# Layer 1 of a two-layer attention and mixture-of-experts kernel: where the shared expert's units stand, and when the experts' weights are sent

## The reference

```python
logits = x @ router_w; scores = sigmoid(logits)
# 4 of 8 groups, then 8 of their experts; weights normed, times 2.5
gate = ragged_dot(xs, w_gate, group_sizes)      # tokens sorted by expert
up   = ragged_dot(xs, w_up, group_sizes)
down = ragged_dot(silu(gate) * up, w_down, group_sizes)
routed = (down[unsort].reshape(T, K, H) * tkw[..., None]).sum(axis=1)
shared = silu(x @ sw_gate) * (x @ sw_up) @ sw_down     # width 256 inside
return routed + shared
```

## Time and profile before

| | us |
|---|---|
| three runs | 1168.87, 1170.13, 1175.76 |
| median | 1170.13 |
| the profiled execution, as timed | 1172.08 |
| its span in the profile | 1169.5 |

### The profile page before, as it was taken

The page is one execution under the profiler, slowest core; times in us unless marked ns, Lnnn a source line. Parts: engine busy times, 40 slices in busy tenths (PEclk is TensorE's granted clock), DMA queues, the critical chain, the costliest instruction groups (busy, mean ns, idle before and its releaser), DMA issues.

```text
span 1169.5 us, 22075 instructions
## 1 busy us (share of the span) xinstructions
PE 899.2 (77%) x5927; PEld 691.8 (59%) x5927; DVE 685.6 (59%) x2692; ACT 467.1 (40%) x1176; POOL 621.2 (53%) x870
## 2 busy tenths in 40 slices
PE   1687989878597992379987888856899999989900
PEld 1465667657355881256665565533688887778700
DVE  4678888865532554467687674352455544444568
ACT  2346666743112441257655443311344444444400
POOL 3646666523163652336558888755356655545500
PEclk9859999988798996559989576787999999999955
DMA  8500000000624543400002222566455655545287
GB/s 231 192 2 1 2 2 1 1 2 1 263 106 127 152 130 120 144 1 2 2 29 86 85 97 101 210 222 221 147 163 174 182 157 161 153 141 156 70 327 319
DMA packets 73093, 136.97 MB, mean 117 GB/s; under 512 B 13406, under 2 KB 51725, under 8 KB 70928
## 3 DMA queue, kind: packets, MB, share of 16 engines
q1 hardware_dynamic: 52144, 85.15, 22.8%
q0 software_dynamic: 17632, 46.73, 11.2%
q10 hardware_dynamic: 3200, 3.70, 0.9%
HBM read 79.15 MB, written 62.39 MB: 121 GB/s over the span
## 4 chain that ended last, share of the span: by engine, by line
PE 36%; DVE 9%; POOL 6%; issue 5%; ACT 2%; another core or an unknown queue 1%; DMA 1%; DVEq 0%; POOLq 0%; ACTq 0%; SPq 0%
PE s_psum L1996 12%; PE s_psum L2009 6%; PE s_psum L1988 3%; POOL rows L1553 3%; PE s_psum L1477 3%; PE s_psum L2004 2%; DVE a_masked L1074 2%; DVE f_rows L2096 2%; DVE f_xT L2096 2%; PE s_psum L549 1%; POOL a_probs L1414 1%; PE s_psum L1496 1%; PE s_psum L646 1%; PE s_psum L602 1%
## 5 line engine op out<-in xcount | busy, mean ns | idle before, releaser
L2106 POOL DMA_INDIRECT parts<-e_y,e_dest x206 | 202.7, 984 | 180.7 <-DVE e_y L2079 96.9
L1996 PE MATMUL s_psum<-wres,e_xT 128*128 x824 | 213.9, 382 | 1.8 <-ACT e_xT L2036 1.0
L1996 PEld LDWEIGHTS s_psum<-wres,e_xT 128*128 128x128 f32 x824 | 156.1, 191 | 26.1 <-issue 5.4
L1414 POOL TENSOR_SCALAR_AFFINE_SELECT a_probs<-a_probs 128x256 f32<-128x256 f32 x256 | 107.5, 444 | 117.6 <-ACT a_probs L870 116.8
L1553 POOL DMA_INDIRECT rows<-f_rows,f_place_at x128 | 125.2, 978 | 40.3 <-issue 31.7
L2009 PE MATMUL s_psum<-wres,e_hT 128*128 x412 | 125.3, 386 | 12.2 <-ACT e_hT L2046 11.6
L870 ACT ACTIVATE a_probs<-s_psum 128x768 f32<-128x768 f32 x128 | 104.6, 817 | 72.8 <-PE s_psum L629 68.2
L2041 ACT ACTIVATE e_act_out<-s_psum 128x128 f32<-128x128 f32 x206 | 57.1, 277 | 180.8 <-PE s_psum L1996 101.6
L2070 DVE TENSOR_TENSOR e_hid<-e_act_out,s_psum 128x128 f32<-128x128 f32 x206 | 59.0, 286 | 91.8 <-issue 42.6
L1074 DVE CUSTOM_DVE_ANT_0 a_masked<-s_psum,a_ahead 128x128 f32<-128x128 f32 (+1 forms) x256 | 76.1, 353 | 42.0 <-PE s_psum L605 39.1
L2079 DVE TENSOR_SCALAR e_y<-s_psum,e_xg 128x256 f32<-128x256 f32 x206 | 99.6, 484 | 0.7 <-issue 0.7
(11 more groups left out here) (297 smaller groups left out, 1993.4 us busy)
## 6 DMA issues: line engine op xcount, KB each, us to landing
e_xg<-rows SPq DMA_DIRECT2D x159, 160.0 KB
f_rows<-parts SPq DMA_DIRECT2D x8, 1024.0 KB, 7.2
f_xT<-parts SPq DMA_DIRECT2D x8, 1024.0 KB, 7.4
wres<-in_experts SPq DMA_DIRECT2D x21, 384.0 KB
e_xg<-rows SPq DMA_DIRECT2D x47, 144.0 KB
wres<-in_experts SPq DMA_DIRECT2D x4, 1536.0 KB
rows<-empty SPq DMA_DIRECT2D x1, 5120.0 KB, 24.1
e_yk<-parts SPq DMA_DIRECT2D x16, 256.0 KB, 2.9
```

The lines of the kernel that those rows point to most:

```text
L1414: last = nc.gpsimd.affine_select(out=diagonal[:, :, a], in_=diagonal[:, :, a], compare_op=ALU.is_ge, fill=0.0, base=0, pattern=[[0, 2], [1 ...
L1996: last = nc.tensor.matmul(ps_u[b % 2][:, 0:2 * P], xT[b % 2][:, c * P:(c + 1) * P], wres[:, ds(e, 1), 2 * c * P:2 * (c + 1) * P].rearrange ...
L2106: nc.gpsimd.indirect_dma_start(out=parts[:, :], out_offset=bass.IndirectOffsetOnAxis(ap=dest[b % NY][:], axis=0), in_=y[b % NY][:], in_off ...
```

## The change

- The tables that placed units 0 to 3 in rounds 9 and 10 are gone. `finish` runs units 0 to 3 in place of 4 to 7. `up(0)` and `up(1)` stand ahead of `count`, so ahead of the wait for the last places.
- Units 4 to 7 (`TAIL_UNITS`) run behind the expert loop: PE behind the last block, ACT ahead of the stores, DVE between the sums of the first eight tiles. Tile 8 waits for all units.
- Attention's buffers are ordered anew, so that parts of `wres` come free earlier. SP sends experts 25 to 13 on one count per slot from (7, 0) to (8, 4), and 12 to 0 on one count per four scatters from round 9 on; the last five also wait for all places. The transfer of five at once is gone.
- In rounds 10 and 11 POOL sends one scatter per slot instead of two, so `finish` has 22 scatters left instead of 6.
- `xg` and `y` of the loop now lie in `rows`, and the four `yk` buffers in `wres`, so that `xT` and the shared weights stay for the last units.

```diff
-PACED = 78
+STACK_EXPERTS, FIRST_QUERY_EXPERTS, SECOND_QUERY_EXPERTS = 19, 16, 13
+ROUND_STEPS = 13
+PACE = 4
+TAIL_UNITS = 4
@@ attention
-        unit_pe = {(B + 1, 0): [("up", 0)], (B + 1, 2): [("up", 1)], (B + 1, 3): [("down", 0)], (B + 1, 5): [("down", 1)],
-                   (B + 1, 7): [("up", 2)], (B + 2, 1): [("up", 3)], (B + 2, 2): [("down", 2)], (B + 2, 6): [("down", 3)]}
@@ sync
-                sp.wait_ge(st_ps, PAIRS * B)
-                sp.wait_ge(max_done, PAIRS * B)
-                for n, e in enumerate(range(FREE_EXPERTS - 1, LAST_EXPERTS - 1, -1)):
+                sp.wait_ge(group_ps, NF * B)
+                for n, e in enumerate(range(FREE_EXPERTS - 1, -1, -1)):
+                    if e == STACK_EXPERTS - 1:
+                        sp.wait_ge(st_ps, PAIRS * (B - 2))
+                    if e == FIRST_QUERY_EXPERTS - 1:
+                        sp.wait_ge(st_ps, PAIRS * (B - 1))
+                    if e == SECOND_QUERY_EXPERTS - 1:
+                        sp.wait_ge(st_ps, PAIRS * B)
+                        sp.wait_ge(max_done, PAIRS * B)
+                    if e == LAST_EXPERTS - 1:
+                        sp.wait_ge(f_placed, B)
                     sp.wait_ge(front["paced"], n + 1)
@@ gpsimd
-                        for _ in range(2):
+                        for _ in range(2 if i <= B + 1 else 1):
...
-                            if scattered >= PACED and scattered % 2:
+                            scattered += 1
+                            if i > B and scattered % PACE == 0:
                                 passed(pool, front["paced"])
-                            scattered += 1
+                        if (B - 1, 0) <= (i, j) < (B - 1 + ROUND_STEPS // PAIRS, ROUND_STEPS % PAIRS):
+                            passed(pool, front["paced"])
@@ finish, tensor
+            units["up"](pe, 0)
+            units["up"](pe, 1)
             count()
-            units["up"](pe, begun)
-            first()
-            units["up"](pe, begun + 1)
-            for u in range(begun, NU):
+            for u in range(end):
                 units["down"](pe, u)
-                if u == begun:
+                if u + 2 < end:
+                    units["up"](pe, u + 2)
+                if u == 0:
+                    first()
+                if u == 1:
                     table()
@@ expert_blocks, tensor, behind the loop
+                units["up"](pe, NU - TAIL_UNITS)
+                units["up"](pe, NU - TAIL_UNITS + 1)
+                for u in range(NU - TAIL_UNITS, NU):
+                    units["down"](pe, u)
+                    if u + 2 < NU:
+                        units["up"](pe, u + 2)
@@ expert_blocks, vector, in the loop over tiles t
+                tail = {0: [("keep", u)], 1: [("keep", u + 1)], 2: [("add", u)], 3: [("keep", u + 2)], 4: [("add", u + 1)],
+                        5: [("keep", u + 3)], 6: [("add", u + 2)], 7: [("add", u + 3)]}
             for t in range(NT):
+                for name, u in tail.get(t, []):
+                    units[name](dve, u)
```

More of the change, by code:

```diff
@@ L391, in attention, with query_homes @@
             place_top = sb("place_top", [P, TB, 8])
+        pieces = NH // 2 + (NK // 2 if multi else 1)
+        def query_homes(i):
+            return (sb(f"qT{i}", [P, PAIRS, N], F32R), sb(f"kT{i}", [P, PAIRS if multi else 1, N], F32R))
+        ahead = sb("ahead", [P, TRI])
+        masked = wide("masked", [P, 2, 2, TRI])
+        max_stack = sb("max_stack", [P, TB, 2, 2 * NH, 2], F32R)
+        maxT = sb("maxT", [P, TRI], F32R)
+        pairs_by_age = {i: query_homes(i) for i in (1, 0, 2)}
+        qT, kT = ([pairs_by_age[i][n] for i in range(NQ)] for n in range(2))
         yT_hi = sb("yT_hi", [P, FC, N], F32R)
@@ L1798, in finish @@
     make_sem, psum, block = shared_stage
-    placed, wres_loaded, units, begun = front["placed"], front["wres_loaded"], front["units"], front["units_begun"]
+    placed, units, end = front["placed"], front["units"], NU - TAIL_UNITS
     with ExitStack() as ctx:
@@ L1887, in _ @@
             dve.wait_ge(ones_made, 1)
+            units["keep"](dve, 0)
             dve.wait_ge(count_ps, 1)
@@ L1892, in _ @@
             nc.vector.tensor_copy(blocks[:], blocks_i[:]).then_inc(blocks_done, 1)
-            units["keep"](dve, begun)
+            units["add"](dve, 0)
+            units["keep"](dve, 1)
             dve.wait_ge(blocks_done, 1)
@@ L1903, in _ @@
             nc.vector.tensor_tensor(lists[:, NB:2 * NB], owned[:], start[:], ALU.mult).then_inc(lists_done, 1)
-            units["add"](dve, begun)
+            units["add"](dve, 1)
+            units["keep"](dve, 2)
             dve.wait_ge(tab_ps, 1)
             nc.vector.tensor_copy(tab[0:1, 0:2 * NB], ps_r[0:1, 0:2 * NB]).then_inc(tab_done, 1)
-            for u in range(begun + 1, NU):
+            units["add"](dve, 2)
+            for u in range(3, end):
                 units["keep"](dve, u)
@@ L2018, in _ @@
             if front is not None:
[L2019 removed]
+                pe.wait_ge(front["units"]["added"], NU - TAIL_UNITS)
             for i in range(NB + 2):
@@ L2029, in _ @@
                     down(i - 2, owner.pop(0))
+            if front is not None:
+                units = front["units"]
+                units["up"](pe, NU - TAIL_UNITS)
[4 more added lines that the diff above has]
+                        units["up"](pe, u + 2)
         @block.scalar
@@ L2056, in _ @@
                     keep_hidden(i - 1)
+            if front is not None:
+                for u in range(NU - TAIL_UNITS, NU):
+                    front["units"]["silu"](act, u)
             if out is not None:
@@ L2090, in _ @@
             sums.start(0)
+            tail = {}
+            if front is not None:
+                units, u = front["units"], NU - TAIL_UNITS
+                tail = {0: [("keep", u)], 1: [("keep", u + 1)], 2: [("add", u)], 3: [("keep", u + 2)], 4: [("add", u + 1)],
+                        5: [("keep", u + 3)], 6: [("add", u + 2)], 7: [("add", u + 3)]}
             for t in range(NT):
+                for name, u in tail.get(t, []):
+                    units[name](dve, u)
+                if front is not None and t == NT // 2:
+                    dve.wait_ge(units["added"], NU)
                 part = yk[t % NC]
```

58 lines of the change are left out of this document (18 added, 40 removed).

## The result

The changed kernel takes 1176.49 us (median of 11 runs, 1169.58 to 1187.07), the kernel before 1166.88 (11 runs, 1159.41 to 1175.76). The ratio is 1.0083, with a 95% interval of 1.0044 to 1.0123: slower by 0.8%. A ratio rests only on executions within 1.5% of the fastest of their kernel, so it can differ a little from the quotient of two medians. Forecast were 1168 us and a gain of 2.2 us. The profiled execution of the changed kernel (1169.95 us, span 1167.9) is one of its fastest, that of before (1172.08, span 1169.5) one of the slower. So the two spans, laid side by side, mislead by about 11 us. Stages have to be compared, and several traces of each kernel.

A forecast was written before the change was run, and what follows sets the result against it. Bounds: POOL in rounds 5 to 8, POOL's scatters beside the routing chain in the drain, PE in the expert loop, DVE in the tail. -14.1 + 11.9 = -2.2 us from 1170.13 gave 1168 us, own range 1162 to 1175.

The forecast's parts named there:

- Part 1, the drain: Rounds 9 and 10 without units: last scatter at 808.4 us, not 822.75, 14.4 us earlier, less 1 us of idle.
- POOL never waits: In the drain, POOL issues its 52 remaining scatters without idling, 1.27 us each, 66.2 us in all.
- perhaps two late starts of about 6 us each: On the path to the places of m=7, late ACT and DVE starts that may disappear, 12 us together.
- the places would stand at about 774 us: The places of m=7 come 12 us sooner on a path of 29.7 us, early enough for POOL.
- 786 with the late starts kept: Time in us of the places of m=7 if ACT and DVE still start late; claimed to fit too.
- Part 2, the loads: Weight loads paced one per slot in rounds 7 and 8, then one per four scatters: DMA share about 0.6, cost 0.
- second rival: Rounds 7 and 8 pay for the loads through late PE or ACT starts: 1180 us, or 1186 with three; chance 0.14.
- No stretch of DMA share above 0.9: Sign expected between rounds 9 and 11, where the near-full DMA stretches should go.
- Part 3, the start: Expert loop's first block near 816 us, effectively 817.3 with a cold PE: 14.1 us ahead of 831.4; ends 6 and 17.
- Begun at 774 they end by 805 and no longer set the start: The four units behind the routing, 31 us at most, finish before the expert loop could start.
- Part 4, the tail: Four units behind the loop: keeps 2.0, adds 4.9, two PE stalls 5.0, sum 11.9 us; ends 8.5 and 15.7.
- third rival: The drain does not shorten fully: late starts return, POOL still idles 8 us; -6 + 12, 1176 us; chance 0.09.

The follow-up runs named there:

- changed_third: The changed kernel unaltered, timed again on one chip in the rounds of the kernels beside it: 1192.17 us, ratio 1.0138 to the kernel before.
- two_units: The changed kernel with the last two of eight units left out, two behind the routing, four behind the loop: 1191.01 us, single time on a slower chip.
- five_tail: The changed kernel with three units behind the routing and five behind the loop, these with banks of their own: 1159.91 us, ratio 0.9955 to the kernel before.
- changed_again: The changed kernel unaltered, run once more for a second trace: 1173.19 us, ratio 1.0064 to the kernel before.
- changed_fourth: The changed kernel unaltered, run once more beside the kernel before in one set: 1171.85 us, ratio 1.0062 to the kernel before.
- hold_scatters: The changed kernel with all scatters from the statistics of m=7 on held until the places of m=7 exist: 1199.7 us, one run.
- spread_units: The changed kernel with units 0 and 1 in round 10, three behind the routing, three behind the loop with own banks: 1184.06 us, ratio 1.0129.
- no_tail_units: The changed kernel with units 4 to 7 behind the loop left out: 1163.18 us, ratio 0.9998 to the kernel before.
- late_scatters: The changed kernel with only the scatters behind attention's last rounds held until the places of m=7; 15 still ran: 1187.07 us, one run.

## Why the prediction was wrong

**Part 1, the drain: the step that failed.** "POOL never waits" held for the statistics of m=7 (no idle time there, where 8.35 us had been). It failed for the places. The prediction let that path lose up(3)'s 5.40 us and "perhaps two late starts of about 6 us each". That subtracted up(3) from a path that it does not lengthen: the path took 31.5 us with up(3) in it and 32.2 to 32.7 without. And it took late starts for an effect of the near-full DMA, which would go with it. The chain from statistics to places did not run 29.7 us because of what lay in it; without scatters beside it it runs 15.1. From POOL's first scatter behind the statistics to the first of m=7 it took 793.50 - 762.99 = 30.5 us, where 29.7 had been and the sum needed 12.3. So "the places would stand at about 774 us" became 792.7, POOL idled 4.07 + 2.23 us, and the drain gave 7 to 9 us of 14.4. "786 with the late starts kept" was in the text, and called early enough; it was still 7 us too early.

**Part 2, the loads: right.** Rounds 7 and 8 stayed at 53.4 to 53.6 us together at DMA shares of 0.70 and 0.53, against 0.6 forecast. The second rival does not occur. "No stretch of DMA share above 0.9" held on the whole, though 765 to 770 us still reaches 0.90; it only didn't bring what it was to bring.

**Part 3, the start: partly wrong.** "Begun at 774 they end by 805 and no longer set the start" hung on the same moment. The units do still hold the start: 9.9, 10.0 and 6.9 us behind the last scatter in three traces of the changed kernel and 15.8 in changed_third, against 6.2 in two_units and five_tail. Last scatter to gather is 2.66 us in two_units, as forecast.

**Part 4, the tail: right, 1.0 to 1.3 us too small.** Three keeps and four adds as counted, and the two waits where they were forecast. Only up behind an idle PE took 6.02 us once and not 5.3. The changed kernel's DVE and PE:

```profile
1112.28 1.22 DVE L1501 TENSOR_TENSOR x<-s_psum,x 128x1024 f32<-128x1024 f32 x1
...
1113.55 6.02 PE L1475 MATMUL s_psum<-f_xT,f_ws 128*128 128x512 f32 x8 [8.57 <-DVE x L1501]
...
1119.67 0.69 DVE L1488 TENSOR_TENSOR u_hid<-s_psum,u_act_out 128x512 f32<-128x512 f32 x1 [3.39 <-PE s_psum L1475]
```

add(4) releases up(6), and keep(6) waits 3.39 us for it; keep(7) waits 2.77 in the same way.

**The sum.** -7 + 13 = +6 us from the stages of changed_again and changed_fourth, where the comparisons gave +7 (changed_fourth) to +10 us (the first set), and +16 on the chip of changed_third, whose trace had the late start of the loop and the long loop besides. This is the third rival, that the drain does not shorten fully, -6 + 12, to which 0.09 was given. It had the size right and the reason half: the late starts came back although the DMA was not full. What was weighed wrongly was evidence of the kernel before: the earlier trace rows shows late starts beside the earlier trace rows, and both lie beside POOL's scatters too. Two causes were present in the same rows, and the prediction took one.

**Still open.** By what way a scatter delays DVE and ACT. In rounds 7 and 8 scatters run too, two per slot with a cut between them, and DVE has no late start over 1.1 us there. Single late starts of 1.18 to 1.23 us come in a row at lines 1173 to 1175, each behind DVE's own instruction before. An instruction block was fetched at 777.8 us in the changed kernel, within DVE's stop of 3.00 us; in hold_scatters one was fetched at 776.4 us and DVE did not stop. That this one fetch waits among the scatters' packets would fit, and was not tested by itself. But fetches are not the general cause: in the longest stops, ACT's of 14.16 us in spread_units (789.1 to 803.3 us) and DVE's of 9.86 us in the kernel before (789.4 to 799.3 us, late from 792.8 on), the profile has no packet of the instruction queues at all. The Trainium skill (Runtime: NRT & Kernel Launch, Instruction fetch mechanics) calls the crossing of a block mostly hidden; hold_scatters agrees, and for the fetch at 777.8 us beside scatters it is open. The Trainium skill (SBUF — State Buffer, SBUF: two separate sides) has DVE and POOL share one port pair, for which DVE's instructions contend that have two inputs in SBUF or run in a two-port mode, and says that ACT never waits for it. It can't be the whole cause: ACT is late by up to 14.16 us, and line 1174, with one input, by 1.19 us. Open is also why no_tail_units was not faster than the kernel before, and why the loss was 1.4% on one chip.

## What to carry to other kernels

A stop that ends with another engine's result is no gain until it is known how long that result's own chain takes alone: take away what runs beside it once (here 32 us became 15), before a cause is named. Work put between the bound engine's instructions costs its own time (here 6.9 us of keeps and adds), and buffers shared with what comes ahead add waits that banks of their own remove (67 us to 59). And where stages of equal code differ by 10 us from one execution to the next, compare stages over several traces, and not two spans.

## What the runs showed of the hardware

- POOL's indirect scatters, back to back every 1.27 us, went with single steps of DVE and ACT that started 1.2 to 6.5 us late (before and changed kernel), once 14.2 us (spread_units, its slowest execution), in the changed kernel at a mean DMA share of 0.30. With the scatters held back (hold_scatters) the same steps followed one another at once. 1.2 and 1.9 us behind the end of the last scatter the late engine started (spread_units, late_scatters).
- 384 KB weight loads beside attention, up to a DMA share of 0.70, did not lengthen a round of about 27 us.
- The expert loop of the same program took 268.9 and 279.5 us in two executions, with PE busy 263.4 and 265.0 us and a granted clock of 0.99 and 1.00; the difference is time in which PE waits.
